# Splitting the rows of the first stage's last loads, and reordering the last transposes and products, in a fused weighted sum, sigmoid and matrix product

## The chip, the cores and the metric

The kernel runs on one core of a Trainium2 chip. The metric is the device time of one execution in microseconds (us); lower is better. The profile is that of one execution, whose own time stands beside its span below.

## What is computed

```python
h = jax.nn.sigmoid(jnp.einsum('bts,st->bs', x, W1) + b1)
return h @ W2.T + b2
```

All arrays are float32: x is (1024, 24, 1024) with axes batch b, step t and feature s, W1 is (1024, 24), W2 is (1024, 1024). x alone is 96 MiB, so most of the work is to read it, to weigh its 24 slices in t and to add them up.

## The kernel before, in words

**Stages.** The (b, s) plane is cut into four quarters of 512 rows by 512 features, one stage each, in the order of `STAGES`. Stages 0 and 1 do rows 0 to 511, stages 2 and 3 rows 512 to 1023; stages 0 and 2 do the first half of the features and their products are kept in `y` ("keep"), stages 1 and 3 do the second half, add to `y` and so finish the output ("last"). A chunk `c` is 128 of a stage's 512 features, a tile is 128 rows by 128 features.

**Two ways to sum over t.** The first 6 or 7 t of a stage (its pool) go through `nat` buffers of 0.5 MiB each, in two halves of rows: POOL multiplies a part with a row of weights (L622) and adds it to the running sum (L630). All other t go through `ring`, five slots of 1 MiB. For these PE transposes tiles into a PSUM bank (L323, `turn_unit`), and DVE multiplies the bank by a column of W1 and adds it to `acc` (L450, `add_unit`). One transposed chunk of one load is a *unit*; it has 4 tiles, or 2 where the load has half of the rows. POOL's two sums enter as units too ("n", PE from `nat`, DVE L448). The list `units` is the order in which PE and DVE take them. Five banks `xbank0` to `xbank4` are used in turn: PE's unit u waits for DVE's unit u-5.

**Split loads.** The fourth number of a stage's row says for how many of its last t the rows come in two parts, first all of the upper halves, then all of the lower ones (0, 0, 9 and 11 t in stages 0 to 3). So the upper half's sums are ready before the stage ends.

**After a chunk's sum.** ACT computes the sigmoid twice, rounded into `h_hi` (L566) and in full into `hbank` (L574); DVE subtracts them into `h_lo` (L465, and L503 in the tail). W2 is turned once in stage 0 (L352) and split the same way. Each output of 128 by 512 is 12 products on PE (h_hi with w_hi and w_lo, h_lo with w_hi, over four chunks; 13 with the bias in "keep"), in `pbank0` and `pbank1` in turn (L394), and is then copied (L552) or added (DVE L484) into `y`. That makes 400 product steps. The table `SPREAD` says where: (stage, first unit, last unit, steps), placed evenly by tiles between the units. What is not placed before the last unit follows behind it: eight steps of the upper half, and then 48 steps in a loop of their own (L427), four outputs in the banks `xbank3, xbank4, xbank0, xbank1`.

**Loads.** SP issues every load in one order. The ring loads follow each other; the nat loads stand before those ring loads whose number is in the stage's list of places. A ring slot is reused when PE has turned the last unit in it, a nat buffer when POOL has added it.

## Time and profile before

| | |
|---|---|
| time, median of 3 runs | 306.85 us (306.82 to 307.05) |
| the profiled execution | 306.58 us, its span 304.8 us |
| busy: PE, DVE, POOL, ACT | 253.5, 245.1, 240.2, 56.8 us |
| moved by DMA | 109.47 MB, 359 GB/s over the span |
| mean granted TensorE clock | 0.964 |

A busy PE counts transposes and products alike; DVE, POOL and PE each are busy for some 80% of the span and the DMA engines for almost all of it until 278 us, so the average does not say what sets the end.

### The profile page before, as it was taken

What the parts mean: (1) busy time and instruction counts of PE and PEld (TensorE: products, weight loads), DVE (VectorE), ACT (ScalarE), POOL (GpSimd) and SP (SyncE); (2) the same over time, 40 slices, a digit from 0 to 9 for tenths busy, and PEclk for the clock granted to TensorE, in tenths of its full rate; (3) what the DMA queues carried; (4) which work ended last, traced back from release to release, by engine and by line L of the source; (5) the groups of instructions that cost most, each with busy time, mean ns of one, the idle gap of its engine ahead of it and who ended that gap; (6) DMA issues with size and microseconds to landing.
All of it is one profiled execution on the core that took longest, in us unless ns stands there. A gap on an engine that the chain in (4) does not pass through costs nothing.

```text
span 304.8 us, 4798 instructions
## 1 busy us (share of the span) xinstructions
PE 253.5 (83%) x1689; PEld 217.5 (71%) x1689; DVE 245.1 (80%) x444; ACT 56.8 (19%) x99; POOL 240.2 (79%) x109
## 2 busy tenths in 40 slices
PE   0295867958879999996676989999949999999995
PEld 0294857948767888886565868888848888877784
DVE  0074995959999888888799879999977889998933
ACT  4040323202254101010060000013140001140040
POOL 2379992958998958999999999997995559989300
PEclk9997997978999999998899999999997999999999
DMA  7999999999999999999999999999999999998103
GB/s 206 396 400 389 388 387 387 398 391 388 387 387 387 385 387 386 387 387 387 387 388 386 387 394 390 395 388 387 387 387 389 390 388 387 385 387 315 71 34 138
DMA packets 55307, 109.47 MB, mean 359 GB/s; under 512 B 3562, under 2 KB 3570, under 8 KB 55284
## 3 DMA queue, kind: packets, MB, share of 16 engines
q1 hardware_dynamic: 54688, 107.06, 95.5%
q10 hardware_dynamic: 596, 2.11, 1.7%
q8 instruction: 13, 0.21, 0.3%
q14 instruction: 10, 0.08, 0.1%
HBM read 104.97 MB, written 4.19 MB: 358 GB/s over the span
## 4 chain that ended last, share of the span: by engine, by line
DMA 36%; PE 36%; POOL 17%; issue 7%; SPq 4%; DVE 1%; POOLq 0%; DVEq 0%
DMA ring<-in_r_x 21%; PE xbank L323 16%; PE pbank L394 14%; POOL nat L630 10%; DMA nat<-in_r_x 9%; POOL nat L622 7%; DMA y<-in_L_rec_W 6%; PE xbank L427 4%; SPq L284 3%; PE pbank L341 1%; SPq L290 1%; PE pbank L352 1%; PE pbank L384 0%; DVE acc L450 0%; DVE y L484 0%
## 5 line engine op out<-in xcount | busy, mean ns | idle before, releaser
L450 DVE SCALAR_TENSOR_TENSOR acc<-xbank,w,acc 128x512 f32<-128x512 f32 (+1 forms) x340 | 195.2, 620 | 30.4 <-PE xbank L323 24.1
L323 PE MATMUL xbank<-ident,ring 128*128 128x128 f32 x1104 | 171.9, 282 | 36.3 <-DMA ring<-in_r_x 29.4
L323 PEld LDWEIGHTS xbank<-ident,ring 128*128 128x128 f32 x1104 | 140.2, 146 | 64.7 <-DVE acc L450 18.8
L622 POOL TENSOR_TENSOR nat<-nat,w1all 128x1024 f32<-128x1024 f32 x54 | 128.4, 2381 | 35.2 <-DMA nat<-in_r_x 28.0
L630 POOL TENSOR_TENSOR nat<-nat 128x1024 f32<-128x1024 f32 x46 | 109.5, 2380 | 3.6
L394 PE MATMUL pbank<-w_hi,h_hi 128*128 128x512 f32 x112 | 51.3, 458 | 0.6 <-ACT h_hi L566 0.5
L394 PE MATMUL pbank<-w_lo,h_hi 128*128 128x512 f32 x112 | 50.2, 448 | 0.0
L394 PE MATMUL pbank<-w_hi,h_lo 128*128 128x512 f32 x112 | 44.8, 450 | 0.0
L566 ACT ACTIVATE h_hi<-acc,b1col 128x256 fp32r<-128x256 f32 (+1 forms) x24 | 13.7, 569 | 84.4 <-DVE acc L450 84.4
L444 DVE TENSOR_SCALAR acc<-xbank,w 128x512 f32<-128x512 f32 x16 | 11.9, 745 | 15.7 <-PE xbank L323 15.6
L552 ACT COPY y<-pbank 128x512 f32<-128x512 f32 x16 | 9.4, 586 | 80.1 <-PE pbank L394 80.1
L394 PEld LDWEIGHTS pbank<-w_hi,h_hi 128*128 128x128 f32 x112 | 21.4, 191 | 1.5 <-ACT h_hi L566 1.3
L394 PEld LDWEIGHTS pbank<-w_lo,h_hi 128*128 128x128 f32 x112 | 21.6, 193 | 0.1
L394 PEld LDWEIGHTS pbank<-w_hi,h_lo 128*128 128x128 f32 x112 | 19.3, 190 | 0.3
L352 PE MATMUL pbank<-ident,y 128*128 128x128 f32 x64 | 11.3, 306 | 7.7 <-DMA y<-in_L_rec_W 6.0
L527 ACT CAST w_hi<-pbank 128x512 fp32r<-128x512 f32 x16 | 9.4, 587 | 41.9 <-PE pbank L352 41.9
L352 PEld LDWEIGHTS pbank<-ident,y 128*128 128x128 f32 x64 | 8.2, 157 | 9.1 <-DMA y<-in_L_rec_W 6.4
L448 DVE TENSOR_TENSOR acc<-xbank,acc 128x256 f32<-128x256 f32 x32 | 12.1, 419 | 2.7 <-PE xbank L323 2.5
L574 ACT ACTIVATE hbank<-acc,b1col 128x256 f32<-128x256 f32 (+1 forms) x24 | 13.1, 545 | 5.1 <-DVE h_lo L465 4.0
L341 PE MATMUL pbank<-ident,w 128*128 128x128 f32 x56 | 10.1, 311 | 3.4 <-DVE w_lo L457 3.4
L323 PE MATMUL xbank<-ident,nat 128*128 128x128 f32 x64 | 11.6, 283 | 0.1
L465 DVE TENSOR_TENSOR h_lo<-hbank,h_hi 128x256 fp32r<-128x256 f32 (+1 forms) x20 | 10.5, 525 | 1.4 <-ACT hbank L574 0.8
(30 smaller groups left out, 91.5 us busy)
## 6 DMA issues: line engine op xcount, KB each, us to landing
ring<-in_r_x SPq DMA_DIRECT2D x49, 1024.0 KB, 13.3
nat<-in_r_x SPq DMA_DIRECT2D x54, 512.0 KB, 12.4
ring<-in_r_x SPq DMA_DIRECT2D x40, 512.0 KB, 12.0
y<-in_L_rec_W SPq DMA_DIRECT2D x2, 2048.0 KB, 18.3
out_y<-y ACTq DMA_DIRECT2D x4, 512.0 KB, 6.3
out_y<-y SPq DMA_DIRECT2D x8, 256.0 KB, 2.1
w<-in_L_rec_W SPq DMA_DIRECT2D x1, 96.0 KB, 2.4
nat<-in_L_rec_b ACTq DMA_DIRECT2D x3, 4.0 KB
```

Of the source, the lines that this page charges most:

```text
L323: mm = pe.transpose(xbank[u % XBANKS][:, a * P:(a + 1) * P], tile, ident[:, :])
L341: mm = pe.transpose(pbank[q % 2][:, a * P:(a + 1) * P], row, ident[:, :])
L352: mm = pe.transpose(pbank[m % 2][:, j * P:(j + 1) * P], y[:, j, c * P:(c + 1) * P], ident[:, :])
L394: mm = pe.matmul(pbank[n % 2][:, :], a[:, c, rows], w[:, STAGES[i][1] + c, cols], start=r == 0, stop=r == per - 1)
L427: mm = pe.matmul(xbank[(UNITS + n - OH * CUT) % XBANKS][:, :], a[:, c, j * P:(j + 1) * P], w[:, STAGES[LAST][1] + c, cols], start=c == 0 a ...
L444: nc.vector.tensor_scalar(total, bank, weight, None, ALU.mult).then_inc(unit_added, 1)
L448: nc.vector.tensor_tensor(total, bank, total, ALU.add).then_inc(unit_added, 1)
L450: nc.vector.scalar_tensor_tensor(out=total, in0=bank, scalar=weight, in1=total, op0=ALU.mult, op1=ALU.add).then_inc(unit_added, 1)
L566: nc.scalar.activation(h_hi[:, c, rows], acc[:, c, rows], ACT.Sigmoid, bias=bias).then_inc(tail_hi if tail else h_hi_ready, 1)
L574: nc.scalar.activation(h_held(i, p), acc[:, c, rows], ACT.Sigmoid, bias=bias).then_inc(h_ready, 1)
L622: nc.gpsimd.tensor_tensor(slot, slot, row, ALU.mult).then_inc(nat_weighed, 1)
L630: nc.gpsimd.tensor_tensor(slot, slot, nat[:, (m - 1) % NATS, :, :], ALU.add).then_inc(nat_added, 1)
```

## The change

Eight edits. (1) The last ten t of stage 0 come in two parts of rows too; in stage 2 it is 12 t instead of 9 and in stage 3 13 instead of 11. (2) The places of the nat loads change, and the units at which POOL's sums enter. (3) `SPREAD` has new numbers: 40 steps now stand in stage 0, 64 in stage 1 (104 before), 129 in stage 2 (126), 119 in stage 3 (114). (4) `units` can take the last loads of a part of a stage by pairs of chunks: first chunks 0 and 1 of all these loads, POOL's sums for them ahead, then chunks 2 and 3 (1 load in stage 1; 4 and 1 in stage 2; 1 and 2 in stage 3). (5) The last 39 units use three banks only (`xbank0` to `xbank2`, PE's unit waits for the DVE unit three back); the last four outputs have `xbank3`, `xbank4`, `pbank0` and `pbank1`. (6) All 352 steps before the last 48 stand ahead of the last unit, none behind. (7) `h_lo` pieces are placed among DVE's units by one rule, also in the tail. (8) W2 is loaded by halves of its columns, 2 KB rows instead of 4 KB, and its 16 turns stand every second unit instead of every third.

```diff
 STAGES = (
-    (0, 0, 6, 0, (8, 17), (0, 0, 0, 0, 2, 7, 8, 11, 11, 12, 14, 15, 16, 17), "keep"),
-    (0, 4, 7, 0, (7, 16), (0, 2, 2, 3, 7, 7, 9, 9, 11, 11, 14, 14, 14, 16, 16, 16), "last"),
-    (4, 0, 7, 9, (9, 22), (2, 3, 6, 6, 6, 8, 10, 13, 14, 16, 20, 23, 25), "keep"),
-    (4, 4, 7, 11, (10, 26), (1, 1, 5, 9, 9, 10, 14, 16, 20, 22, 22), "last"),
+    (0, 0, 6, 10, (9, 18), (0, 0), (2, 3, 4, 4, 6, 6, 8, 8, 10, 10, 10, 15, 15, 16, 20, 20, 20, 21, 26), "keep"),
+    (0, 4, 7, 0, (5, 16), (1,), (0, 3, 4, 5, 6, 14, 14, 15, 16), "last"),
+    (4, 0, 7, 12, (15, 26), (4, 1), (0, 2, 2, 5, 5, 10, 10, 12, 14, 18, 20, 25, 26, 26, 27), "keep"),
+    (4, 4, 7, 13, (11, 28), (1, 2), (2, 3, 5, 7, 10, 13, 17, 18, 22, 24, 25), "last"),
 )
 SPREAD = (
...
-    (3, 6, 38, 36),
-    (3, 25, 71, 35),
-    (3, 76, 88, 17),
-    (3, 87, 111, 26),
+    (0, 84, 119, 40),
...
+    (3, 5, 29, 29),
+    (3, 18, 71, 39),
+    (3, 73, 117, 45),
+    (3, 120, 125, 3),
+    (3, 115, 127, 3),
 )
...
+            for first, last, groups in ((start, end - pairs, 1), (end - pairs, end, 2)):
+                ns = [f for f in range(2) if first <= STAGES[i][4][f] < last]
+                for q in range(groups):
+                    cs = range(q * NC // groups, (q + 1) * NC // groups)
+                    if groups > 1:
+                        order += [("n", 0, c, HALF * f, HALF) for f in ns for c in cs]
...
+                        order += [("x", t, c, row, n) for c in cs]
...
+    NARROW = 39
+    FREE = XBANKS - 2
...
+    def xbank_of(u):
+
+        return u % XBANKS if u < UNITS - NARROW else (u - UNITS + NARROW) % FREE
+
...
+        def tail_bank(n):
+
+            if NARROW == 0:
+                return xbank[(UNITS + n) % XBANKS]
+            return xbank[FREE + n] if n < 2 else pbank[n - 2]
...
-                if u >= XBANKS:
-                    pe.wait_ge(unit_added, u + 1 - XBANKS)
+                if last_in_bank(xbank_of(u), u):
+                    pe.wait_ge(unit_added, last_in_bank(xbank_of(u), u))
...
+            def tail_step(step):
...
+                elif c == 0 and k == 0:
+
+                    pe.wait_ge(y_added, added_at[LAST] + OH * CUT + n - 3)
...
-                    if splits[i] and row == 0:
-                        u = part_end(i) + 2 + 2 * c
-                    else:
-                        u = first_unit[i + 1] + c
+                    narrow = int(splits[i] > 0 and (sums[i][p][1] == 0 or i == LAST))
+                    u = min(UNITS, max(u + 1 + narrow, sum_end(i, p) + 3 + 2 * narrow))
...
-                        sp.dma_start(y[:, :, :], w2_v[0]).then_inc(w2_loaded[0], 16)
+                        sp.dma_start(w2_half, w2_v[:, :, :BANK]).then_inc(w2_loaded[0], 16)
...
-        W2S = {10 + 3 * m if m < SC else 52 + 3 * (m - SC): m for m in range(OH * SC)}
+        W2S = {11 + 2 * m if m < SC else 56 + 2 * (m - SC): m for m in range(OH * SC)}
```

The order of the instructions shows what this does to the end of the program. First PE of before, from the first transpose of POOL's last sum (`nat`, `ident` is the identity matrix) to the first products of the last four outputs; "x16" are eight units of two tiles.

```order
L323 MATMUL xbank<-ident,nat 128x128 x2
L394 MATMUL pbank<-w_lo,h_hi 128x512
L323 MATMUL xbank<-ident,nat 128x128 x2
L394 MATMUL pbank<-w_hi,h_hi 128x512
L323 MATMUL xbank<-ident,nat 128x128 x2
L394 MATMUL pbank<-w_lo,h_hi 128x512
L323 MATMUL xbank<-ident,nat 128x128 x2
L323 MATMUL xbank<-ident,ring 128x128 x16
L394 MATMUL pbank<-w_hi,h_hi 128x512
...
L394 MATMUL pbank<-w_hi,h_lo 128x512 x4
L427 MATMUL xbank<-w_hi,h_hi 128x512 x4
```

Here 11 steps of the upper half (three between the nat units, eight at the end) stand between POOL's last sum and the last four outputs. Now the same stretch of PE in the changed kernel (L364 are transposes, L463 products of the upper half, L416 those of the last four outputs).

```order
L364 MATMUL xbank<-ident,nat 128x128 x2
L463 MATMUL pbank<-w_hi,h_hi 128x512
L364 MATMUL xbank<-ident,nat 128x128 x2
L364 MATMUL xbank<-ident,ring 128x128 x4
L463 MATMUL pbank<-w_lo,h_hi 128x512
L364 MATMUL xbank<-ident,ring 128x128 x2
L463 MATMUL pbank<-w_hi,h_lo 128x512
L364 MATMUL xbank<-ident,ring 128x128 x2
L463 MATMUL pbank<-w_hi,h_lo 128x512
L364 MATMUL xbank<-ident,nat 128x128 x4
L463 MATMUL pbank<-w_hi,h_lo 128x512 x2
L364 MATMUL xbank<-ident,ring 128x128 x8
```

The 24 transposes are the same in number (8 of nat, 16 of ring), six steps stand among them instead of 11 among and behind them, and chunks 2 and 3 come as a group at the end. DVE of before in the same stretch (L448 adds POOL's sums, L484 finishes an output in `y`):

```order
L484 TENSOR_TENSOR y<-pbank,y 128x512
L448 TENSOR_TENSOR acc<-xbank,acc 128x256 x4
L450 SCALAR_TENSOR_TENSOR acc<-xbank,w,acc 128x256 x8
L503 TENSOR_TENSOR h_lo<-hbank,h_hi 128x256 x4
L484 TENSOR_TENSOR y<-pbank,y 128x512
```

And DVE of the changed kernel there (L498 adds POOL's sums, L500 the weighted tiles, L531 finishes an output, L515 makes `h_lo`):

```order
L498 TENSOR_TENSOR acc<-xbank,acc 128x256 x2
L500 SCALAR_TENSOR_TENSOR acc<-xbank,w,acc 128x256 x4
L498 TENSOR_TENSOR acc<-xbank,acc 128x256 x2
L500 SCALAR_TENSOR_TENSOR acc<-xbank,w,acc 128x256
L531 TENSOR_TENSOR y<-pbank,y 128x512
L500 SCALAR_TENSOR_TENSOR acc<-xbank,w,acc 128x256
L515 TENSOR_TENSOR h_lo<-hbank,h_hi 128x256
L500 SCALAR_TENSOR_TENSOR acc<-xbank,w,acc 128x256 x2
L515 TENSOR_TENSOR h_lo<-hbank,h_hi 128x256 x3
```

The twelve adds are the same; one addition into `y` and the first `h_lo` have moved in between the last of them.

## Rows read from the trace of the kernel before

**Rows 1.** The page: busy tenths, granted clock and DMA in 40 slices.
```profile
PE   0295867958879999996676989999949999999995
DVE  0074995959999888888799879999977889998933
POOL 2379992958998958999999999997995559989300
PEclk9997997978999999998899999999997999999999
DMA  7999999999999999999999999999999999998103
```

**Rows 2.** Windows: busy us and count of each engine, clock, DMA share, GB/s.
```profile
110.00:120.00 10.00, 10.00 (x68) 8.53 (x67) 8.24 (x14) 0.59 (x1) 9.01 (x4) 1.00 1.05 387
250.00:260.00 10.00, 10.00 (x71) 8.54 (x69) 9.18 (x23) 1.17 (x2) 9.84 (x6) 1.00 1.05 387
278.00:279.00 1.00, 1.00 (x8) 0.81 (x7) 1.00 (x3) 0.00 (x0) 1.00 (x1) 1.00 0.82 311
281.00:282.00 1.00, 1.00 (x8) 0.79 (x7) 1.00 (x4) 0.00 (x0) 1.00 (x1) 1.00 0.49 176
283.00:284.00 1.00, 1.00 (x10) 0.86 (x8) 1.00 (x4) 0.00 (x0) 1.00 (x1) 1.00 0.09 33
```

**Rows 3.** Timeline of PE: where it waited for a ring load after 220 us.
```profile
227.94 2.33 PE L323 MATMUL xbank<-ident,ring 128*128 128x128 f32 x12 [4.00 <-DMA ring<-in_r_x]
235.69 0.63 PE L323 MATMUL xbank<-ident,ring 128*128 128x128 f32 x4 [0.22 <-DMA ring<-in_r_x]
242.41 0.63 PE L323 MATMUL xbank<-ident,ring 128*128 128x128 f32 x4 [0.23 <-DMA ring<-in_r_x]
```

**Rows 4.** The chain that ended last, from 284.85 us: start, us, what.
```profile
284.85 0.10 issue
284.95 0.41 PE xbank L323 x2
285.36 0.23 PE pbank L394
285.59 0.22 PE xbank L323 x2
...
286.50 2.35 PE xbank L323 x18
288.84 1.85 PE pbank L394 x8
290.69 10.89 PE xbank L427 x48
301.59 0.02 issue
301.61 0.69 DVE y L484
```

**Rows 5.** Timeline of POOL, its last operations.
```profile
270.33 2.39 POOL L622 TENSOR_TENSOR nat<-nat,w1all 128x1024 f32<-128x1024 f32 x1 [0.97 <-DMA nat<-in_r_x]
...
282.43 2.38 POOL L630 TENSOR_TENSOR nat<-nat 128x1024 f32<-128x1024 f32 x1
```

**Rows 6.** Timeline of DVE, near the end.
```profile
271.27 0.41 DVE L465 TENSOR_TENSOR h_lo<-hbank,h_hi 128x256 fp32r<-128x256 f32 x1
271.60 3.22 DVE L450 SCALAR_TENSOR_TENSOR acc<-xbank,w,acc 128x256 f32<-128x256 f32 x8
...
285.09 0.68 DVE L484 TENSOR_TENSOR y<-pbank,y 128x512 f32<-128x512 f32 x1
285.69 1.49 DVE L448 TENSOR_TENSOR acc<-xbank,acc 128x256 f32<-128x256 f32 x4
287.09 3.22 DVE L450 SCALAR_TENSOR_TENSOR acc<-xbank,w,acc 128x256 f32<-128x256 f32 x8
```

**Rows 7.** Timeline of DVE in stage 0: three adds of 512 columns.
```profile
32.95 2.06 DVE L450 SCALAR_TENSOR_TENSOR acc<-xbank,w,acc 128x512 f32<-128x512 f32 x3
```

**Rows 8.** Groups of lines with shapes apart, 242 to 291 us.
```profile
L450 DVE SCALAR_TENSOR_TENSOR acc<-xbank,w,acc 128x256 f32<-128x256 f32 x88 | 36.7, 478 | 2.2 <-PE xbank L323 2.2
```

**Rows 9.** The page: DMA issues, KB each, median us to landing.
```profile
ring<-in_r_x SPq DMA_DIRECT2D x49, 1024.0 KB, 13.3
ring<-in_r_x SPq DMA_DIRECT2D x40, 512.0 KB, 12.0
```

145 lines of the change are left out of this document (76 added, 69 removed).

## The prediction, made before the changed kernel was run

> **What bounds the kernel now.** I first read the 40 slices [rows 1]. The DMA engines are at 9 from the second slice to 278 us or so, so up to there the time is that of the bytes: no engine makes the stream faster, it can only hold it up. The total of the loads is the same in both kernels (the 96 MiB of x once, W2 once), so the stream ends where it ended, between 283 and 284 us, where the share is 0.09 [rows 2]. The span is 304.8 us. What can be won is in the 21 us behind the stream, and what can be lost is there or in a hole in the stream.
>
> Next the waits of PE for loads, late in the kernel [rows 3]. The last one of any size ends at 227.94 (4.00 us), then come 0.22 and 0.23 us at 235.69 and 242.41, and none behind. From 242.41 PE has more work than time. PE is full in its windows, with a granted clock of 1.00 [rows 2], and so there is no slow clock to win back.
>
> Then the chain at the end [rows 4]. At 284.85 something releases PE, and it takes up POOL's last sum. From 284.95 to 301.59 PE never rests: three upper-half products among the 8 transposes of nat, then 16 transposes of ring, at 288.84 eight more upper-half products (1.85 us), at 290.69 the 48 products of the last four outputs (10.89 us). Behind it one addition of DVE (0.69 us) and a store; span end minus PE's end is 304.8 - 301.59 = 3.2 us.
>
> What released PE at 284.85 is read from POOL [rows 5]. It waits for a nat load until 270.33, and from there six operations follow each other (three parts, each multiplied and added); the last one runs from 282.43 to 284.81. That is the moment at which PE goes on. DVE is about as late: it works from 285.09 without a rest, and its last add ends at 287.09 + 3.22 = 290.31 [rows 6]. So three engines arrive together, and PE's remaining work is what the time is made of.
>
> **The change part by part, at the end.** POOL first. The nat load that POOL waits for at 270.33 is the third last. In stage 3 it stood ahead of ring load 20 and now stands ahead of ring load 22; because two more t are split, the bytes ahead of it are the same in both (95.1 MiB by counting the loads). The last two come 1.5 and 0.5 MiB later than they did, at 387 GB/s [rows 2] some 4 and 1.4 us, but POOL takes 4.8 us a part and still finds them landed. So POOL's last sum is again made at 284.8, and PE can't take it up earlier. I take this as fixed.
>
> PE from there on. Before: 24 transposes and 3 + 8 upper-half steps from 284.95 to 290.69, 5.74 us [rows 4]. Now: the same 24 transposes, and 6 steps. Five steps fewer at 1.85 / 8 = 0.231 us are 1.16 us, so the 48 products begin at 289.5. The five steps haven't vanished, they stand earlier in stage 3 and the stages before it. At 242 us, by equal tiles, the changed kernel is 12 steps further (263 against 251), because PE had 4 us to spare before 227.94 [rows 3]. These moved steps cost nothing only because PE waited for loads there; if that cover were gone, they'd cost 0.23 us each.
>
> DVE, the same stretch. It can begin with POOL's sum at about 285.3 (transposes 0.41 us, rows 4). It has four sums (285.69 to 287.09, 1.40 us), eight adds (3.22 us), and now also one addition into y (285.09 to 285.69, 0.60) and one h_lo (271.27 to 271.60, 0.33) [rows 6]. That ends at 290.9, against 290.31 before. But the last four outputs don't wait for DVE's end now: with the pairs of chunks, chunk 0 is complete seven units earlier, and PE's last transposes only need DVE's unit three back. From there to DVE's end lie 0.60 + 0.40 + 0.33 + 0.80 = 2.1 us, and PE needs some 0.5 us from release to its first product. So DVE allows a start at 290.9 - 2.1 + 0.5 = 289.3. Both engines say about the same; I take PE's 289.5. h_hi and h_lo of chunks 1 to 3 are wanted 2.7 us apart (12 products), and DVE and ACT made them 1 us apart before, so they hide. The fourth output's bank `pbank1` waits for the addition into y, which stands 1.5 us before DVE's end and so is done as PE comes to it.
>
> Sum: 289.5 + 10.89 + 3.2 = 303.6 for a span of 304.8, a gain of 1.2 us. The profiled execution took 306.58, so this is 305.4 by that clock. The median of before is 0.27 above its profiled execution, so I forecast 305.6.
>
> **Does DVE get there in time?** This is what the gain depends on. A split load costs DVE more: two adds of 256 columns at 3.22 / 8 = 0.403 us [rows 6] make 0.81, against 2.06 / 3 = 0.69 for one of 512 [rows 7], so 0.12 more. Stage 3 has 8 such pairs more, 1.0 us. Counted from the load that landed at 235.69 [rows 3], which is stage 3's fourth in both kernels with the same bytes ahead: PE then has 40 tiles at 0.11 us (0.22 for two, rows 4) and 25 steps at 0.23, 10.2 us, before the half loads come where DVE is the slower one, so at 245.9. From 246.3 DVE has 84 adds (33.9 us), four of POOL's sums (1.4), four h_lo (1.3) and three additions into y (1.8): 284.7. That is 0.6 us ahead of 285.3. So it is in time, if it never waits. In before its 88 adds there were preceded by 2.2 us of waiting for PE [rows 8]. With three banks in place of five, PE can be fewer units ahead, and each addition into y (0.60 us) eats that lead. Between 0 and 2.2 us of waiting, DVE would be 0.6 early or 1.6 late. I take its arrival as just on time, nearer to the lower end, because almost every unit in this stretch now has a product beside it (45 steps over 44 units), so PE isn't far ahead at any time anyway and doesn't stall in bursts.
>
> **The edits elsewhere.** Stage 0 gets 20 half loads for 10 whole ones, 40 pairs of adds for 40 adds, 5 us of DVE work; DVE's slices there stand between 4 and 9 [rows 1] and it waits for loads, so it costs nothing. Its 40 early steps fill slices where PE is at 5 to 8. W2 by column halves moves the same 4 MiB in rows of 2 KB, as x has them (a chunk group of 512 float32); nothing. Its turns stand closer together, still behind the landing of their loads. More, smaller loads: 70 of 512 KB and 34 of 1 MiB instead of 40 and 49. The rate was 387 GB/s in a window of whole loads and 387 in one of half loads [rows 2], so this costs nothing while the queue is full; if it isn't, the next rival says what.
>
> The Trainium skill speaks against this edit: its page "DMA: Bandwidth & Descriptors", section "Measured (HBM→SBUF, 128 partitions, SWDGE, issued from GpSimd)", says to batch DMAs to at least 1 MiB for 75% of peak. By that rule the half loads of stages 2 and 3 should already have moved at a lower rate, and this trace doesn't agree: 387 and 387.
>
> **Rivals.**
> *DVE eats it up* (chance 0.20). It waits for PE as it did, 2.2 us, and is 1.6 us late at POOL's sum. The gain of 1.2 becomes a loss of 0.3: 306.3 to 307.2. For it: DVE's tenths are 7 to 9 in slices 31 to 38 [rows 1], the busiest stretch next to PE's. Against it: PE is the later engine there.
> *A hole in the stream in stage 2* (0.10, ends slower). Four half loads are turned by pairs of chunks, so their two ring slots come free only when the 20 units of that group (40 tiles, 25 steps, 10.1 us at the paces above) are done, some 6 to 7 us later than by single loads. From issue to landing a load takes 12.0 to 13.3 us [rows 9], so about 6 us of queue remain. In the tail, where nothing new is issued, the share sinks from 0.82 to 0.09 between 278 and 284 [rows 2]: the engines run dry at different times, at about half of the rate over 6 us. A hole of that kind costs up to 2.8 us, all of it on the path: 308.4. It decides from 1.8 us on. Against it: the queue isn't empty, only thinner.
> *The half loads are slower after all* (0.01, the rule above as a mechanism): a stream 1% slower would be 2.8 us, again 308.4.
> *Three banks stall PE at every addition into y, beyond DVE's lateness* (0.07, slower): four times 0.6 us, 307.8.
> *Everything on time and more* (0.12, faster): POOL's sum or DVE comes 0.5 to 1.2 us sooner, 304.4 to 305.1. The floor is the last load at 284: 16 transposes, 53 steps and 3.2 us behind it give 301.2, 303.3 by the median; POOL's six operations stand in the way.
>
> **Numbers.** The forecast's own case has 0.50 (304.9 to 306.2). A change under 0.2%, 0.6 us, can't be told from none in this kernel. Faster: 0.50 + 0.12 = 0.62. Same: 0.20. Slower: 0.10 + 0.01 + 0.07 = 0.18. The range goes from 304.4 to 307.3; it leaves out most of the two slower cases and little below.
>
> **What would show it.** Right: POOL's last operation ends near 284.8 again, PE's transposes of POOL's last sum begin within 0.5 us of it, the 48 products begin near 289.5 and run 10.9 us unbroken; DMA at 387 GB/s between 180 and 215 us; DVE's waits for PE after 245 us under 2 us. Wrong: a GB/s figure under 380 in a slice of stage 2; DVE's last add after 292; PE waiting for `acc` again and again in its last 39 units; or POOL's third last part starting at a time other than 270.3, since the sum is hung on that.

## The result, and the profile after

The changed kernel takes 308.86 us (median of 6 runs, 308.12 to 310.1), the kernel before beside it 306.89 us (6 runs, 306.65 to 307.05). The ratio is 1.0069 with a 95% interval of 1.0057 to 1.008, so the change makes the kernel some 2 us slower (1.97 by the medians, 2.1 by the ratio). The forecast was 305.6 us, a gain of 1.2. The six times of the changed kernel lie in two groups, three at 308.1 to 308.4 us and three at 309.3 to 310.1, and the profiled execution, at 309.87 us with a span of 308.1, is one of the upper three; so its rows tell where time stands, they overstate the loss by about 1.0 us, and sizes are taken from the ratios below.

First the page of the changed kernel in 40 slices, in answer to [rows 1].

```profile
PE   0946769388999888996658999999994999999995
...
DVE  0555997579999988996795899999996689999953
...
POOL 3519999999999999109999989795998786989200
PEclk9996998869999999999995999999998699999999
DMA  7999999999999999999999999999999999996103
GB/s 208 374 387 387 386 386 387 385 387 387 386 386 387 385 387 387 387 388 385 387 387 387 386 394 389 396 387 387 389 384 405 387 383 385 383 387 252 40 35 136
```

The DMA row has no hole, as before. DVE stands at 9 in slices 10 to 14 and again in 17 and 18, where stage 0's half loads are added and behind them. PEclk has two dips in the later half, a 5 in slice 22 and an 8 and a 6 in slices 31 and 32 (231 to 246 us). The GB/s are 374 to 388 in the slices 2 to 22, nowhere more.

Next the waits of PE for loads from 160 us on (the first is at the end of stage 1), and the moment at which it takes up POOL's last sum, in its timeline (start, us, what, and in brackets the idle time before it).

```profile
162.91 1.94 PE L364 MATMUL xbank<-ident,ring 128*128 128x128 f32 x8 [3.24 <-DMA ring<-in_r_x]
...
230.68 0.63 PE L364 MATMUL xbank<-ident,ring 128*128 128x128 f32 x4 [0.23 <-DMA ring<-in_r_x]
...
238.28 1.09 PE L364 MATMUL xbank<-ident,ring 128*128 128x128 f32 x4 [4.02 <-DMA ring<-in_r_x]
...
289.27 0.38 PE L364 MATMUL xbank<-ident,nat 128*128 128x128 f32 x2
...
293.69 0.71 PE L416 MATMUL xbank<-w_hi,h_hi 128*128 128x512 f32 x2
```

[Rows 3] had the long wait at 227.94, before stage 3. Now there is next to none there, but one of 4.02 us at 238.28, for stage 3's fourth load (before, that load was awaited for 0.22 us and used at 235.69). Behind it four transposes take 1.09 us instead of 0.63: the granted clock is at the lower of its two levels, 1.2 in place of 2.4 GHz. The windows around it (busy us and count of PE, PEld, DVE, ACT, POOL, then clock, DMA share, GB/s):

```profile
230.00:240.00 10.00, 5.75 (x33) 4.44 (x31) 6.37 (x10) 0.59 (x1) 7.86 (x4) 0.85 1.05 400
240.00:250.00 10.00, 10.00 (x55) 8.42 (x54) 6.80 (x14) 0.59 (x1) 9.11 (x4) 0.81 1.05 387
250.00:260.00 10.00, 10.00 (x71) 8.61 (x70) 9.55 (x25) 1.18 (x2) 7.05 (x4) 1.00 1.04 382
```

In 240 to 250 PE is busy all the time at a mean clock of 0.81, so it does a fifth less than at 1.00. In windows of 2 us the clock is seen to fall still inside the wait and to stay at half for some 6.8 us, from 237.0 to 243.8:

```profile
236.00:238.00 2.00, 0.00 (x0) 0.00 (x0) 0.00 (x0) 0.00 (x0) 2.00 (x1) 0.74 1.04 405
238.00:240.00 2.00, 1.72 (x6) 1.47 (x7) 0.60 (x1) 0.00 (x0) 0.01 (x1) 0.50 1.06 396
240.00:242.00 2.00, 2.00 (x10) 1.81 (x9) 0.90 (x2) 0.00 (x0) 1.27 (x1) 0.50 1.05 387
242.00:244.00 2.00, 2.00 (x9) 1.70 (x8) 0.75 (x1) 0.00 (x0) 1.92 (x2) 0.55 1.05 386
```

From 244 to 304.86 PE is never idle: whatever it is late by at 244 it is late by at the end.

POOL's last operations, in answer to [rows 5]:

```profile
272.69 2.39 POOL L665 TENSOR_TENSOR nat<-nat,w1all 128x1024 f32<-128x1024 f32 x1 [0.68 <-DMA nat<-in_r_x]
...
284.76 2.39 POOL L673 TENSOR_TENSOR nat<-nat 128x1024 f32<-128x1024 f32 x1
```

The third last part starts at 272.69, not 270.33, and the last sum is made at 284.76 + 2.39 = 287.15, not 284.81. PE takes it up only at 289.27, 2.1 us after it was there. The 48 products start at 293.69 and end at 304.86. DVE, in answer to [rows 6]:

```profile
293.36 0.68 DVE L531 TENSOR_TENSOR y<-pbank,y 128x512 f32<-128x512 f32 x1
...
294.35 0.41 DVE L515 TENSOR_TENSOR h_lo<-hbank,h_hi 128x256 fp32r<-128x256 f32 x1
294.68 0.86 DVE L500 SCALAR_TENSOR_TENSOR acc<-xbank,w,acc 128x256 f32<-128x256 f32 x2
...
304.20 1.37 DVE L531 TENSOR_TENSOR y<-pbank,y 128x512 f32<-128x512 f32 x2
```

DVE's last add ends at 294.68 + 0.86 = 295.54, and the last addition into y stands in the row at 304.20.

### The profile page after: what moved, and what is told of

Read it like the earlier page. It is cut to its first block, busy times and chain, and to the rows that moved or that the text cites. A ratio compares the mean times of both kernels' runs of the same rounds, so it can differ in the third digit from the quotient of the medians.

```text
span 308.1 us, 4975 instructions
## 1 busy us (share of the span) xinstructions
PE 258.3 (84%) x1689; PEld 218.1 (71%) x1689; DVE 251.4 (82%) x508; ACT 58.7 (19%) x107; POOL 239.8 (78%) x109
## 4 chain that ended last, share of the span: by engine, by line
PE 47%; DMA 41%; SPq 4%; DVE 4%; issue 3%; DVEq 0%
DMA ring<-in_r_x 41%; PE xbank L364 23%; PE pbank L463 18%; DVE acc L500 3%; SPq L325 2%; PE xbank L416 2%; PE pbank L416 2%; SPq L331 1%; PE pbank L453 1%; PE pbank L393 1%; DVE w_lo L507 1%; SPq L337 0%; DVE y L531 0%; DVE acc L498 0%; SPq L334 0%
## 5 line engine op out<-in xcount | busy, mean ns | idle before, releaser
L500 DVE SCALAR_TENSOR_TENSOR acc<-xbank,w,acc 128x256 f32<-128x256 f32 (+1 forms) x400 | 201.7, 557 | 35.6 <-PE xbank L364 34.0
L364 PE MATMUL xbank<-ident,ring 128*128 128x128 f32 x1104 | 185.0, 284 | 40.8 <-DMA ring<-in_r_x 38.5
L364 PEld LDWEIGHTS xbank<-ident,ring 128*128 128x128 f32 x1104 | 143.4, 146 | 73.6 <-issue 26.8
L463 PE MATMUL pbank<-w_hi,h_hi 128*128 128x512 f32 x112 | 54.0, 482 | 0.0
L463 PE MATMUL pbank<-w_lo,h_hi 128*128 128x512 f32 x112 | 52.7, 471 | 0.0
L463 PE MATMUL pbank<-w_hi,h_lo 128*128 128x512 f32 x112 | 49.4, 473 | 0.0
L613 ACT ACTIVATE h_hi<-acc,b1col 128x256 fp32r<-128x256 f32 (+1 forms) x28 | 14.9, 531 | 80.2 <-DVE acc L500 80.1
L463 PEld LDWEIGHTS pbank<-w_hi,h_hi 128*128 128x128 f32 x112 | 21.8, 195 | 0.3 <-ACT y L600 0.2
L463 PEld LDWEIGHTS pbank<-w_lo,h_hi 128*128 128x128 f32 x112 | 22.0, 196 | 0.0
L463 PEld LDWEIGHTS pbank<-w_hi,h_lo 128*128 128x128 f32 x112 | 20.5, 193 | 0.0
L498 DVE TENSOR_TENSOR acc<-xbank,acc 128x256 f32<-128x256 f32 x32 | 12.6, 418 | 1.5 <-PE xbank L364 1.3
L515 DVE TENSOR_TENSOR h_lo<-hbank,h_hi 128x256 fp32r<-128x256 f32 (+1 forms) x28 | 12.6, 452 | 1.4 <-ACT hbank L618 1.1
L364 PE MATMUL xbank<-ident,nat 128*128 128x128 f32 x64 | 12.1, 289 | 0.6 <-DVE acc L500 0.6
L507 DVE TENSOR_TENSOR w_lo<-pbank,w_hi 128x512 fp32r<-128x512 f32 x16 | 10.8, 678 | 0.0
```

The source lines that it names most:

```text
L364: mm = pe.transpose(xbank[xbank_of(u)][:, a * P:(a + 1) * P], tile, ident[:, :])
L463: mm = pe.matmul(pbank[n % 2][:, :], a[:, c, rows], w[:, STAGES[i][1] + c, cols], start=r == 0, stop=r == per - 1)
L498: nc.vector.tensor_tensor(total, bank, total, ALU.add).then_inc(unit_added, 1)
L500: nc.vector.scalar_tensor_tensor(out=total, in0=bank, scalar=weight, in1=total, op0=ALU.mult, op1=ALU.add).then_inc(unit_added, 1)
L507: nc.vector.tensor_tensor(w_lo[:, c, cols], pbank[m % 2][:, :], w_hi[:, c, cols].bitcast(F32), ALU.subtract).then_inc(w_lo_ready, 1)
L515: nc.vector.tensor_tensor(h_lo[:, c, rows], h_held(i, p), h_hi[:, c, rows].bitcast(F32), ALU.subtract).then_inc(h_lo_ready, 1)
```

## Experiments

Each kernel ran in 5 rounds beside the kernel before, whose medians were 306.81, 307.0, 306.77 and 306.79 us in the four groups; differences between kernels are those of their ratios to it, times 306.8 us. An interval is 0.0008 to 0.0017 to either side, by 5 to 12 executions of the kernel, so two ratios tell 0.4 to 0.6 us apart and no less.

### Parts of the change undone

**w2_rows**: the changed kernel, with W2 loaded by halves of its rows again (4 KB rows).

```diff
-    w2_v = W2.rearrange("(j p) s -> p j s", p=P)
+    w2_v = W2.rearrange("(h j p) s -> h p j s", p=P, j=JT)
...
-                        sp.dma_start(w2_half, w2_v[:, :, :BANK]).then_inc(w2_loaded[0], 16)
+                        sp.dma_start(y[:, :, :], w2_v[0]).then_inc(w2_loaded[0], 16)
```

> The changed kernel, but W2 is loaded by halves of its rows (4 KB a row) as before. Theory A (the stream is on the path: the changed kernel moved about 0.43 MB less in its first 69 us, with 374 to 387 GB/s in slices where before had 396 to 400) expects slices near 396 again and every later landing about 1.1 us sooner, so 1.1 us less than the changed kernel's median of 308.86: 307.8. Theory B (only the last 70 us count, DVE and the three banks) expects no difference: 308.9.

Measured: 307.97 us, ratio 1.0033 [1.0021, 1.0045], 1.1 us less than the changed kernel, as theory A has it. POOL's third last part starts at 271.77. The wait for stage 3's fourth load is as long as in the changed kernel's trace (4.01 us, until 237.26) and the clock is halved behind it too, but only until 240.1 us, for 3.4 us in all:

```profile
237.26 1.09 PE L364 MATMUL xbank<-ident,ring 128*128 128x128 f32 x4 [4.01 <-DMA ring<-in_r_x]
...
238.00:240.00 2.00, 2.00 (x9) 1.70 (x8) 0.75 (x1) 0.00 (x0) 0.28 (x1) 0.50 1.05 387
240.00:242.00 2.00, 2.00 (x14) 1.64 (x13) 1.74 (x3) 0.00 (x0) 2.00 (x1) 0.97 1.05 388
```

**fill**: the 29 steps at the start of stage 3 stand in units 4 to 13 instead of 5 to 29.

```diff
-    (3, 5, 29, 29),
+    (3, 4, 13, 29),
```

> The changed kernel, but the 29 product steps that stood evenly over units 5 to 29 of stage 3 stand over units 4 to 13. PE sat idle for 4.02 us before load 3 of stage 3 landed at 238.28, and then ran at about half of its clock until 244. Theory A (PE's backlog from that landing on sets the end) expects some 14 steps (3.2 us) done inside the idle time, the clock at 1.00, another 2.6 us back: 304 to 305.5, limited by DVE. Theory B (DVE and three banks at the end set it) expects at most 0.5 us: 308.4 or more. If the landing is what counts and PE's work isn't, the same.

Measured: 307.48 us, 1.0023 [1.0014, 1.0032], 1.4 us less. That lies between the two theories, 304 to 305.5 and 308.4 or more. The timeline of PE:

```profile
237.62 0.63 PE L364 MATMUL xbank<-ident,ring 128*128 128x128 f32 x4 [1.72 <-DMA ring<-in_r_x]
...
286.71 0.41 PE L364 MATMUL xbank<-ident,nat 128*128 128x128 f32 x2 [0.42 <-POOL nat L673]
```

Stage 3's fourth load comes 0.7 us sooner, which isn't the edit's doing (it is used at 237.49 in the run wide, too). The wait for it has shrunk from 4.02 to 1.72 us, since PE has products to do while the load is on its way, and the clock stays at 1.00 behind it. And PE now waits for POOL's sum (0.42 us at 286.71) instead of coming late to it. So PE was the later of the two in the trace of the changed kernel, and here POOL is.

**wide**: five banks to the end, and the last four outputs in xbank banks as before.

```diff
-    NARROW = 39
+    NARROW = 0
```

> The changed kernel, but the last 39 units use five banks as all others, and the last four outputs the banks that come free last. Theory B (three banks make PE and DVE wait for each other, about 2.5 us in the last 30 us) expects 306.4 to 307.4. Theory A expects 308.2 to 308.9, since PE's work behind load 3 of stage 3 is unchanged.

Measured: 308.59 us, 1.0057 [1.0045, 1.0069]; 0.4 us less, within the error, as theory A has it. The trace tells why it is so little (rows of PE's timeline with POOL's last sum among them, then windows):

```profile
237.49 0.63 PE L364 MATMUL xbank<-ident,ring 128*128 128x128 f32 x4 [3.93 <-DMA ring<-in_r_x]
...
284.13 2.39 POOL L673 TENSOR_TENSOR nat<-nat 128x1024 f32<-128x1024 f32 x1
...
286.67 0.41 PE L364 MATMUL xbank<-ident,nat 128*128 128x128 f32 x2
...
291.82 0.50 PE L416 MATMUL xbank<-w_hi,h_hi 128*128 128x512 f32 x1 [0.47 <-DVE acc L500]
292.54 0.50 PE L416 MATMUL xbank<-w_hi,h_hi 128*128 128x512 f32 x1 [0.23 <-DVE acc L500]
```

```profile
238.00:240.00 2.00, 2.00 (x10) 1.57 (x9) 1.07 (x2) 0.00 (x0) 0.00 (x0) 0.55 1.05 387
240.00:242.00 2.00, 2.00 (x12) 1.70 (x10) 1.18 (x2) 0.00 (x0) 1.97 (x1) 0.59 1.06 390
```

PE is at POOL's last sum at 286.67 and not at 289.27, but most of that isn't the banks: up to the last 39 units both kernels issue the same instructions, and still the fourth load is used 0.8 us sooner here and the clock is at half for 3.4 us and not for 6.8. From the fourth load to POOL's last sum PE takes 49.2 us here (286.67 - 237.49) and 49.7 in w2_rows (286.99 - 237.26), which has three banks and as short a stretch of half clock; so the banks are worth some 0.5 us up to there. Then the products of the last outputs start in banks in which DVE's adds aren't done, and wait for them twice. DVE was busy for 10.00 us of 10 in 260 to 270 and in 270 to 280 in both kernels; its last add ends at 292.88 here. From DVE's last add to the end of the span it is 13.4 us here (306.3 - 292.88), and 12.6 in the changed kernel (308.1 - 295.54): the own banks do save 0.8 us behind DVE.

**nopairs**: no loads by pairs of chunks.

```diff
-    (4, 4, 7, 13, (11, 28), (1, 2), ...
+    (4, 4, 7, 13, (11, 28), (0, 0), ...
```

> The changed kernel, but no loads are taken by pairs of chunks: every load's four chunks follow each other. Theory C (ring slots held by the group of four loads in stage 2 make later loads late) expects load 3 of stage 3 to land 1 to 2.6 us sooner and 306.5 to 308. Theory A with PE's backlog as the cause of the late slot expects the same landing within 0.5 us and a loss of up to 1 us at the end, where the pairs let PE start its last products early: 308.9 to 309.9.

Measured: 309.44 us, 1.0085 [1.0069, 1.0101]. That is theory A's range. The pairs don't cost; they may give 0.5 us, which the intervals leave open. The fourth load of stage 3 is used at 237.37 after 3.67 us of waiting, and at 237.49 with the pairs in wide, so the hole in the stream by the pairs (the second rival) isn't there.

### Parts of the change alone, on the kernel before

**before_w2cols**: the kernel before with W2 by halves of its columns.

```diff
-                        sp.dma_start(y[:, :, :], w2_v[0]).then_inc(w2_loaded[0], 16)
+                        sp.dma_start(w2_half, w2_v[:, :, :BANK]).then_inc(w2_loaded[0], 16)
```

> The kernel before with one edit: W2 is loaded by halves of its columns (rows of 2 KB instead of 4 KB), all else at its place. Theory A (the stream is on the path, and W2 in 2 KB rows moves at 387 GB/s where 4 KB rows gave slices of 391 to 400) expects 0.6 to 1.0 us more than before: 307.4 to 307.9. The rival, that the 0.9 us that the changed kernel gained from the reverse edit came from something that only exists there (PE's lateness), expects no change, 306.8.

Measured: 307.55 us, 1.0023 [1.0014, 1.0032], 0.7 us more than before, theory A. The GB/s of the slices, first of the kernel before and then of this one:

```profile
GB/s 206 396 400 389 388 387 387 398 391 388 387 387 387 385 387 386 387 387 387 387 388 386 387 394 390 395 388 387 387 387 389 390 388 387 385 387 315 71 34 138
```

```profile
GB/s 212 395 387 387 385 386 387 384 387 387 386 387 387 383 387 387 387 386 387 386 387 385 388 392 392 396 386 386 387 386 399 388 387 387 385 387 304 74 35 137
```

W2's halves move in the slices 3 and 8 to 9. There the kernel before has 400 and 398, 391; by columns it is 387 and 384, 387. Of the other full slices only one differs by more than a few GB/s: slice 31, with 399 here against 389, where stores of the output go out beside the loads. The columns lose where W2 moves, 13, 14 and 4 GB/s over 7.6 us each, 0.24 MB or 0.6 us at 387. POOL's third last part starts at 271.16, 0.8 us later than in [rows 5]. The edit changes two things at once: the rows are half as long, and they no longer follow each other in memory. Which of the two costs isn't shown.

**tail_alone**: the changed code with all tables of before (no split of stage 0, W2 by rows), so only the edits of the tail: three banks, own banks, pairs in stage 3, eight steps ahead of the last unit instead of behind it.

```diff
     (3, 87, 111, 26),
+    (3, 111, 119, 8),
...
+    NARROW = 39
```

> The changed code with all tables of before (splits, places of the nat loads, spread of the steps, W2 by rows), so that only the end differs: the eight last steps of the upper half stand ahead of the last unit, the last two loads go by pairs of chunks, the last 39 units use three banks and the last four outputs have banks of their own. My sum for the end, applied here, expects up to 1.2 us less than before (305.6), since the steps stand ahead of POOL's last sum or beside it. The rival, that steps moved ahead of that sum make PE and DVE later there by as much, expects 306.5 to 307.1.

Measured: 307.9 us, 1.0033 [1.002, 1.0045], 1.0 us more than before, above both expectations. POOL's third last part is late by half a microsecond only (270.81, and 270.73 in tail_fivebanks below). PE's only wait behind 270 us is a new one, just behind the start of the last four outputs:

```profile
291.28 0.40 PE L414 MATMUL pbank<-w_hi,h_hi 128*128 128x512 f32 x1
292.36 0.50 PE L414 MATMUL pbank<-w_hi,h_hi 128*128 128x512 f32 x1 [0.68 <-DVE y L529]
```

The third output's product in pbank0 starts on time at 291.28; the fourth's, in pbank1, waits for an addition into y that DVE has only just made (from 291.62, 0.68 us). The first twelve products take 3.80 us by it, until 294.53, where before they take 2.72 (290.53 to 293.25), and the rest goes at the pace of before.

**tail_fivebanks**: the same with five banks and the last outputs in xbank banks.

```diff
-    NARROW = 39
+    NARROW = 0
```

> The changed code with all the tables of before, as in the run with the tail alone (307.9 us, 0.9 more than before), but five banks to the end in place of three, and the last four outputs in xbank3, xbank4, xbank0 and xbank1 as before. Theory A (three banks are the dearer part: PE is held closer to DVE): 306.9 to 307.3 us. Theory B (the steps and additions that moved into the last units, and the pairs, cost it, whatever the number of banks): 307.6 to 308.1 us.

Measured: 306.59 us, 0.9992 [0.9984, 1.0001]: 1.3 us less than tail_alone, and below both expectations. With the tables of before the banks, three of them and the last outputs' own, are all of the tail's cost.

**steps_moved**: the kernel before with one row more in its table.

```diff
     (3, 87, 111, 26),
+    (3, 111, 119, 8),
```

> The kernel before with one line more in its table: the eight upper-half steps that followed the last unit stand between units 111 and 119 of stage 3 instead. Theory A (the prediction's: moved steps are free, and those that get ahead of POOL's last sum shorten PE's way behind it, at 0.23 us each): 305.0 to 306.2 us. Theory B (PE has no idle time in this stretch and reaches POOL's sum later by what was moved ahead of it, so nothing is won): 306.7 to 307.2 us. Theory C (the additions into y that the moved steps need fall among the last adds of DVE, 0.6 us each, and hold PE up): 307.4 to 308.0 us.

Measured: 306.52 us, 0.999 [0.9982, 0.9999], hardly below before. None of the eight steps came to stand ahead of POOL's last sum: PE takes it up at 284.99 (284.95 before) and does the same 24 transposes and 11 steps behind it, only mixed. The 48 products start at 290.22, and by the same view at 290.53 before. So this run doesn't test what the prediction did with such steps, only that mixing them in does no harm. Theory C is refuted, and 306.52 lies between theories A and B.

### Stage 0

**stage0_whole**: the changed kernel with stages 0 and 1 as before: no split, the old places of the nat loads, the old early steps, no pair in stage 1, W2's turns at their old units. Two nat loads that stood first in stage 2's list stand in stage 1 again. W2 by columns stays.

```diff
-    (0, 0, 6, 10, (9, 18), (0, 0), (2, 3, 4, 4, 6, 6, 8, 8, 10, 10, 10, 15, 15, 16, 20, 20, 20, 21, 26), "keep"),
-    (0, 4, 7, 0, (5, 16), (1,), (0, 3, 4, 5, 6, 14, 14, 15, 16), "last"),
+    (0, 0, 6, 0, (8, 17), (0,), (0, 0, 0, 0, 2, 7, 8, 11, 11, 12, 14, 15, 16, 17), "keep"),
+    (0, 4, 7, 0, (7, 16), (0,), (0, 2, 2, 3, 7, 7, 9, 9, 11, 11, 14, 14, 14, 16, 16, 16), "last"),
...
-    (0, 84, 119, 40),
-    (1, 4, 63, 64),
+    (1, 2, 53, 104),
```

> The changed kernel with stages 0 and 1 as before: no split loads in stage 0, its 40 steps back in stage 1 (104 there), nat loads of these stages at their old places, W2's turns at their old units. W2 stays by columns. If the split of stage 0 and what goes with it costs something (waits of 5.20 us at 62 us and 3.24 us at 163 us with a halved clock behind it), this is 0.5 us or more faster than the changed kernel: 307.5 to 308.4. If everything that isn't the stream is recovered before stage 3, it is the same within 0.3 us: 308.9.

Measured: 306.71 us, 0.9998 [0.9989, 1.0007]: 2.2 us less than the changed kernel, the dearest part of all, and more than the 0.5 to 1.4 us that was expected. Here POOL sets the end: its last sum is made at 283.47 + 2.38 = 285.85, and PE waits for it.

**split_only**: the same, but stage 0 split, with places that have the same bytes ahead of them.

```diff
-    (0, 0, 6, 0, (8, 17), (0,), (0, 0, 0, 0, 2, 7, 8, 11, 11, 12, 14, 15, 16, 17), "keep"),
+    (0, 0, 6, 10, (8, 26), (0, 0), (0, 0, 0, 0, 2, 7, 8, 14, 14, 16, 20, 22, 24, 26), "keep"),
```

> The changed kernel with stages 0 and 1 as before except that the last ten t of stage 0 still come in two parts of rows; W2 by columns. The same with stage 0 whole took 306.7 us, with all the edits of stages 0 and 1 308.9. Theory A (the split itself does it: DVE pays two adds for one, 5 us more, and reaches stage 1 late): 308.0 to 309.0 us, and a wait of PE of 2 to 4 us between 155 and 165. Theory B (the places of the nat loads and the early steps of stages 0 and 1 do it): 306.4 to 307.2 us.

Measured: 308.36 us, 1.0058 [1.0041, 1.0075]. Of the 2.2 us the split is 1.8, as theory A has it; the new places, early steps and units of W2's turns are 0.3, within the error. The wait of 2 to 4 us between 155 and 165 that theory A expected isn't there (the longest is 1.25 us, at 162.58). Windows of stage0_whole and then of split_only, where stage 0's last loads are worked on:

```profile
40.00:50.00 10.00, 5.59 (x39) 4.62 (x38) 8.43 (x15) 1.66 (x4) 5.03 (x3) 0.86 1.05 386
50.00:60.00 10.00, 10.00 (x76) 10.00 (x75) 6.61 (x11) 4.32 (x8) 8.46 (x4) 0.80 1.05 386
60.00:70.00 10.00, 7.56 (x62) 6.42 (x61) 9.40 (x16) 1.17 (x2) 6.08 (x4) 1.00 1.05 387
70.00:80.00 10.00, 5.81 (x50) 5.15 (x48) 9.23 (x15) 2.35 (x4) 9.84 (x5) 1.00 1.05 387
80.00:90.00 10.00, 7.41 (x61) 6.60 (x62) 9.06 (x16) 3.43 (x5) 9.53 (x5) 1.00 1.05 387
```

```profile
40.00:50.00 10.00, 8.14 (x62) 6.63 (x63) 10.00 (x19) 1.61 (x3) 5.96 (x3) 1.00 1.05 387
50.00:60.00 10.00, 9.28 (x76) 7.78 (x74) 9.11 (x23) 5.43 (x10) 2.19 (x1) 1.00 1.05 385
60.00:70.00 10.00, 7.93 (x59) 6.36 (x60) 9.95 (x22) 3.61 (x7) 9.77 (x6) 1.00 1.05 387
70.00:80.00 10.00, 8.31 (x42) 4.07 (x41) 10.00 (x27) 4.79 (x9) 9.84 (x5) 1.00 1.05 387
80.00:90.00 10.00, 9.45 (x55) 5.46 (x55) 10.00 (x27) 1.25 (x3) 9.92 (x5) 1.00 1.05 386
```

DVE is busy for 42.7 us of these 50 with stage 0 whole and for 49.1 with it split; in three of the five windows it has not a moment left. The GB/s are the same. Up to 230 us DVE has 4.8 us more of work (190.83 against 186.02). Much later, stage 3's fourth load is awaited until 236.71 in the one (3.03 us) and until 237.87 in the other (4.00 us). Behind the shorter wait the clock stays at 1.00, behind the longer it is at half for 3.4 us:

```profile
238.00:240.00 2.00, 2.00 (x11) 1.70 (x10) 0.75 (x1) 0.00 (x0) 0.00 (x0) 0.61 1.05 389
240.00:242.00 2.00, 2.00 (x9) 1.63 (x9) 1.28 (x2) 0.00 (x0) 1.66 (x1) 0.54 1.06 389
```

At the end the products of the last outputs start at 292.26 in place of 290.45, 1.8 us later: 0.95 because POOL's last sum is made later (284.41 + 2.39 = 286.80), the rest because PE comes 1.0 us late to it.

**small_loads**: stage0_whole, with the last ten loads of stage 0 issued as two of 512 KB each; work and order stay whole.

```diff
+    def in_two(i, t):
+        return i == 0 and t >= T - 10
...
-                    sp.dma_start(ring[:, use % RING, sub * n:(sub + 1) * n, :],
+                    pieces = 2 if in_two(i, t) else 1
+                    for q in range(pieces):
+                        a, b = q * n // pieces, (q + 1) * n // pieces
+                        sp.dma_start(ring[:, use % RING, sub * n + a:sub * n + b, :],
```

> The kernel with stage 0 whole (306.7 us, W2 by columns), but the last ten loads of stage 0 are each issued as two of 512 KB into the same slot, one for either half of the rows; the engines' work, its order and the units stay whole. Theory A (the split costs through the engines' work, two adds for one on DVE and the order of the units): 306.4 to 307.1 us. Theory B (more and smaller loads move less or land later by themselves): 307.6 to 308.6 us, and ring loads awaited 1 us later than in the run with stage 0 whole (236.7).

Measured: 306.68 us, 0.9999 [0.9991, 1.0008], the same as stage0_whole. The smaller loads are free in stage 0; what is left of the split is the engines' work and its order. The trace isn't the same all along: PE is busy for 4.00 of 4 us between 234 and 238, so the fourth load of stage 3 isn't awaited at all. In both runs PE waits for POOL's last sum (until 286.23 and 286.00), and that sets the end.

**split_five**: split_only with five t in two parts.

```diff
-    (0, 0, 6, 10, (8, 26), (0, 0), (0, 0, 0, 0, 2, 7, 8, 14, 14, 16, 20, 22, 24, 26), "keep"),
+    (0, 0, 6, 5, (8, 21), (0, 0), (0, 0, 0, 0, 2, 7, 8, 11, 11, 12, 15, 17, 19, 21), "keep"),
```

> As in the run with the split alone (308.4 us against 306.7 with stage 0 whole), but the last five t of stage 0 come in two parts of rows in place of ten. Theory A (each added pair of adds costs its DVE time, 20 pairs in place of 40): half of the loss, 307.3 to 307.8 us. Theory B (DVE has slack that five t fit into and ten do not): 306.5 to 307.0 us. Theory C (the split delays whatever its size, since the stage's first-half sums and its products move): 308.0 to 308.6 us.

Measured: 307.09 us, 1.0011 [1.0003, 1.002], 0.4 us above stage0_whole. It lies between theories A and B: the first half of the split costs a quarter of the whole, with an error as large as itself. W2's second half is also turned at other units here, which wasn't tried apart.

**before_split**: tail_fivebanks (306.59 us) with the split of stage 0, W2 by rows.

```diff
-    (0, 0, 6, 0, (8, 17), (0,), (0, 0, 0, 0, 2, 7, 8, 11, 11, 12, 14, 15, 16, 17), "keep"),
+    (0, 0, 6, 10, (8, 26), (0, 0), (0, 0, 0, 0, 2, 7, 8, 14, 14, 16, 20, 22, 24, 26), "keep"),
```

> The changed code with the tables of before and five banks (306.6 us) and one part of the change added: the last ten t of stage 0 in two parts of rows. Theory (the split costs 1.0 to 2.0 us wherever it stands): 307.6 to 308.6 us, POOL's third last part at 271.5 to 272.5 in place of 270.7. Rival (it costs only together with W2 by columns, which already thins the stream there): 306.3 to 307.1 us.

Measured: 307.2 us, 1.0012 [1.0004, 1.0021]. The split costs 0.6 us there, between theory and rival. POOL's third last part isn't late (270.55, and it finds the load landed), so this part of the theory is refuted: here PE waits 1.37 us for a ring load at 278.34, where in tail_fivebanks it waited 0.42 us, for DVE. It takes up POOL's last sum at 285.86, 0.9 us after it is made (282.61 + 2.38 = 284.99).

### Several parts undone together

**w2_fill**: w2_rows and fill together; the edits are those two.

```diff
-    w2_v = W2.rearrange("(j p) s -> p j s", p=P)
+    w2_v = W2.rearrange("(h j p) s -> h p j s", p=P, j=JT)
...
-    (3, 5, 29, 29),
+    (3, 4, 13, 29),
```

> The changed kernel with two edits undone or mended: W2 by rows as before (alone -0.9 us) and the 29 steps of stage 3 over units 4 to 13 (alone -1.4 us). If the two are independent, as theory A has it (stream, and PE's idle time before load 3 of stage 3), they add up: 306.4 to 306.8. If both only shorten the same wait, the result is that of the better one, 307.5.

Measured: 306.95 us, 1.0001 [0.9992, 1.0009], 2.1 us less than the changed kernel, where the sum of the two is 2.5. The difference is within the error, so these two may well add up.

**whole_w2_fill**: stage0_whole, w2_rows and fill together, so w2_fill and also:

```diff
-    (0, 0, 6, 10, (9, 18), ...
-    (0, 84, 119, 40),
-    (1, 4, 63, 64),
+    (0, 0, 6, 0, (8, 17), ...
+    (1, 2, 53, 104),
```

> The changed kernel with three parts undone: stages 0 and 1 as before (no split, old places of the nat loads, old early steps), W2 by halves of rows, 29 steps of stage 3 from unit 4 to 13 in place of 5 to 29. Theory (three separate losses that add up: about 2.1, 0.9 and 1.4 us of 308.9): 304.0 to 305.2 us, the third last part of POOL at 270.3 to 270.9, ratio to before 0.990 to 0.995. Rival (all three cure the same lateness, so the second and third add nothing once the stream is on time): 306.2 to 307.0 us, ratio 0.998 to 1.000.

Measured: 306.0 us, 0.9974 [0.9962, 0.9986], 0.8 us faster than before and the fastest of all kernels here. Both expectations miss it: the three parts make 4.7 us one by one (1.1, 1.4, 2.2) and 2.9 together. The ratio of the changed kernel stands in all four numbers, so the difference of 1.8 us is known to some 1.0 us only. First POOL's rows, then PE's:

```profile
270.62 2.39 POOL L663 TENSOR_TENSOR nat<-nat,w1all 128x1024 f32<-128x1024 f32 x1
...
282.69 2.38 POOL L671 TENSOR_TENSOR nat<-nat 128x1024 f32<-128x1024 f32 x1
```

```profile
285.21 0.41 PE L363 MATMUL xbank<-ident,nat 128*128 128x128 f32 x2 [0.47 <-POOL nat L671]
...
289.67 0.71 PE L414 MATMUL xbank<-w_hi,h_hi 128*128 128x512 f32 x2
```

POOL's sum is made at 282.69 + 2.38 = 285.07, PE waits for it, and the products start 289.67 - 285.21 = 4.46 us later. Why the losses overlap is argued from how late PE is at POOL's sum: 2.1 us in the changed kernel, 1.0 in split_only, 0.8 in w2_rows (286.99 against 286.22), and not at all in fill and stage0_whole. fill and stage0_whole each take all of this lateness away, by themselves, and it can be won only once; from there on only what makes POOL earlier counts. w2_rows shows nothing of the kind: PE works at half clock for 5.5 us in the changed kernel's one trace (238.3 to 243.8) and for 2.9 there (237.3 to 240.1), and half of that difference, 1.3 us, is all that PE is earlier at POOL's sum.

**whole_w2_fill_wide**: that with five banks.

```diff
-    NARROW = 39
+    NARROW = 0
```

> As the run with three parts undone (306.0 us), and also five banks to the end and the last four outputs in xbank banks. Theory A (three banks cost what they cost on the tables of before, 1.3 us, once nothing else is late): 304.6 to 305.4 us. Theory B (POOL's last sum sets the end there, and three banks cost nothing behind it): 305.7 to 306.3 us. Theory C (without the banks of their own the last outputs wait for DVE's last adds, as in the run with five banks, 0.5 to 0.7 us): 306.4 to 307.0 us.

Measured: 306.63 us, 0.9995 [0.9987, 1.0004], 0.6 us more: theory C. PE waits for POOL's last sum (0.72 us, until 285.50). Here too the first products of the last outputs wait for DVE's adds, by 0.45 and 0.22 us. So three banks and own banks cost 1.3 us with the tables of before, give 0.6 here, and in the changed kernel cost 0.4, which is within the error.

## Why the prediction was wrong

**What held.** The working behind POOL's last sum. The 48 products start 293.69 - 289.27 = 4.42 us after PE takes it up (4.46 in whole_w2_fill); before it is 5.58 by the same view, so 1.16 us are won, and the prediction had 1.16. They run for 11.2 us without a rest (11.1 before by this view), and 3.2 us lie behind them. The pairs of chunks made no hole in the stream: no slice from 180 to 215 us is under 387 GB/s. Smaller loads are free, as small_loads shows for stage 0. The rule of the Trainium skill's page "DMA: Bandwidth & Descriptors", section "Measured (HBM→SBUF, 128 partitions, SWDGE, issued from GpSimd)", to batch DMAs to at least 1 MiB isn't borne out by this kernel's full queue, as the prediction said: 306.68 against 306.71 us.

**"5 us of DVE work; DVE's slices there stand between 4 and 9 [rows 1] and it waits for loads, so it costs nothing."** This step failed, and it is the dearest. The size of the work was right (5 us forecast, 4.8 more in split_only up to 230 us), the cover was not there: a row of tenths from 4 to 9 doesn't say that 5 us more fit between a load's landing and the next one's, and the same row has four slices at 9 in a row, 10 to 13, right behind. DVE became the full engine of stage 0's second half. It costs 1.8 us with W2 by columns and the other edits, 0.6 us on the tables of before. Shown is that the size of the loads isn't the cause. The last part of the way to the end is shown, too: a later fourth load in stage 3, a halved clock behind it, and POOL's last sum 0.95 us later. Not shown is why that load is used 1.16 us later. The GB/s up to 230 us are 382 in both, but this is rounded to 1 GB/s, which leaves up to 0.6 us open.

**"W2 by column halves moves the same 4 MiB in rows of 2 KB, as x has them [...]; nothing."** This failed too: 0.7 us alone and 1.1 us in the changed kernel. The bytes are the same, the rate isn't. The prediction read 387 GB/s from two windows of x loads and never looked at the slices in which W2 moves, where the page of before had 400 and 398. A stream that is the bound was taken as fixed, while the change touched what is in it.

**"I take this as fixed"** (POOL's third last part at 270.33). It was 272.69, and 271.16 from W2's columns alone. The same number of bytes stood ahead, but they moved later. As the prediction said, its sum was hung on that: 2.36 us in the trace. Some 0.6 of it belong to this one execution, whose stream was thin from the start: 208 and 374 GB/s in its first two slices, where wide, with the same loads in the same order, has 223 and 390 and POOL's part at 272.05. (The prediction also misread what follows: the second last nat load stands behind two half loads in both kernels, so it isn't 1.5 MiB later. It bears on nothing, since POOL finds it landed.)

**"These moved steps cost nothing only because PE waited for loads there" (the 4.00 us before 227.94).** The condition was right and the reading of where the idle time would be was not. The steps filled the idle time before 227.94, but the next idle time then stood at 234 to 238 us, 4.02 us, inside stage 3, where `(3, 5, 29, 29)` has its steps spread evenly up to unit 29, most of them behind the fourth load; and it brought a halved clock with it, which the prediction left out ("there is no slow clock to win back"). The kernel before had one already, for 3.4 us behind its own wait of 4.00 us (the 7 in slice 31 of PEclk, [rows 1]):

```profile
228.00:230.00 2.00, 2.00 (x13) 2.00 (x13) 1.29 (x2) 0.00 (x0) 2.00 (x1) 0.61 1.04 398
230.00:232.00 2.00, 2.00 (x9) 1.60 (x7) 0.96 (x2) 0.00 (x0) 1.92 (x2) 0.54 1.04 418
```

The change moved it 10 us nearer to the end, into the stretch from which PE never rests again. Where it stood before it was covered even at twice the length: tail_fivebanks has 6.8 us of half clock behind its wait until 228.25 and is in time for POOL's sum, at 306.59 us. PE is 2.1 us late at POOL's sum in the changed kernel's trace (half clock for 6.8 us), and 1.0, 0.8, 0.6 and 0.15 in split_only, w2_rows, nopairs and wide (3.4 us each). Half clock for 3.4 us more costs up to 1.7 us; that this is what parts the upper three times of the changed kernel from the lower three is likely, but there is a trace of one of them only. fill undoes wait and half clock by the place of the 29 steps alone, for 1.4 us. The Trainium skill's page "TensorE: Matmul & The Clock Gate", section "HAM oscillation — how this bites in real kernels", has it that a wait of PE for a DMA can bring the clock down, so that the work behind it starts at the lower one; the trace agrees, with a clock of 0.50 from 237.0 on, inside the wait of 4.02 us.

**DVE's arrival.** The first rival was in part what happened. DVE was idle for only 1.3 us from 245 to 290 us and full from 260 to 280, but its last add ended at 295.54, past the 292 that the prediction named as a sign of being wrong. It had its idle moments before 251.5 us and none from there to 289.6, so it could not make up for what the half clock had cost; which of the two engines sets the pace in that stretch isn't shown, as neither waits for the other by more than 0.2 us. In wide and whole_w2_fill_wide it is DVE's adds that the last outputs wait for. The fourth rival (three banks stall PE) priced 2.4 us at four additions; on the tables of before it is 1.3 us, at one addition into y (a wait of 0.68 us, and the first twelve products 1.1 us longer). That is the bank `pbank1` of which the prediction said that its addition "is done as PE comes to it"; in the changed kernel's own trace it is.

**The sum.** In the trace the 48 products start at 293.69, where 289.5 was forecast: POOL's sum is 2.34 us later (287.15), PE comes 2.1 us late to it, and from there on the forecast holds within 0.2 us. By the ratios, with the three losses taken out (whole_w2_fill), what is left of the change is -0.8 us, of -1.2 forecast; with them it is +2.1. The gap of 3.3 us to the forecast is then 2.9 us for steps that were costed at nothing, and 0.4 us for a gain that was smaller, which is no more than the error; 0.26 of it is POOL's sum, at 285.07 still later than 284.81.

## What to carry to other kernels

Where a stream of loads is the bound, look at its rate in the slices in which the very transfer that is edited moves; how its rows lie is part of the rate. Work that is put into an engine's idle time needs a gap that is there in the trace of the changed kernel: idle time moves when it is filled, so ask where the next wait will be and keep spare products just ahead of it. Losses that make the same engine late don't add up, and have to be measured together as well as one by one. And before a number is read from one trace, see where that execution lies among the others of its kernel: here 1.0 us above the median, in a half clock that lasted twice as long.
